# Column tiles of 32 for the masked products, and TensorE's block of 32 steps written out without an inner loop

## The reference

```
def step(St, inp):
    qt, kt, vt, gt, bt = inp
    St = St * jnp.exp(gt)[..., None]
    err = jnp.einsum('bhk,bhkv->bhv', kt, St)
    St = St + bt[..., None, None] * kt[..., None] * (vt - err)[..., None, :]
    ot = jnp.einsum('bhk,bhkv->bhv', qt, St)
    return (St, ot)
_, o = jax.lax.scan(step, S0, (qs, ks_, vs, gs, bs))
```

## Time and profile before

| | us |
|---|---|
| median of 3 runs | 9948.8 |
| lowest, highest of them | 9948.15, 9957.26 |
| the profiled execution: its own time | 9947.83 |
| its span in the trace | 9946.0 |
| TensorE (PE) busy | 9259.0 |
| VectorE (DVE) busy | 7394.6 |
| ScalarE (ACT) busy | 6812.3 |
| GpSimd (POOL) busy | 3586.7 |

### The profile page before, as it was taken

The page is one execution under the profiler, slowest core; times in us unless marked ns, Lnnn a source line. Parts: engine busy times, 40 slices in busy tenths (PEclk is TensorE's granted clock), DMA queues, the critical chain, the costliest instruction groups (busy, mean ns, idle before and its releaser), DMA issues. The chain is left out here.

```text
span 9946.0 us, 369852 instructions
## 1 busy us (share of the span) xinstructions
PE 9259.0 (93%) x137172; PEld 6223.8 (63%) x137172; DVE 7394.6 (74%) x13320; ACT 6812.3 (68%) x15797; POOL 3586.7 (36%) x5963
## 2 busy tenths in 40 slices
PE   4799999999999999999999999999999999997888
PEld 2566666666666666666666666666666666663333
DVE  2688888888888888888888888888888888872111
ACT  1677777777777777777777777777777777771111
POOL 0344434444343443443434444443434344440000
PEclk7899999999999999999999999999999999998999
DMA  0211111111111111111111111111111111110000
GB/s 28 52 39 37 39 36 39 37 38 38 36 38 37 39 37 36 38 37 36 39 37 38 38 37 38 36 39 36 39 37 39 36 38 37 37 53 17 8 8 13
DMA packets 514021, 351.68 MB, mean 35 GB/s; under 512 B 63137, under 2 KB 510753, under 8 KB 512817
## 3 DMA queue, kind: packets, MB, share of 16 engines
q1 hardware_dynamic: 511760, 328.31, 13.1%
q0 software_dynamic: 1088, 4.26, 0.1%
HBM read 289.94 MB, written 42.47 MB: 33 GB/s over the span
## 5 line engine op out<-in xcount | busy, mean ns | idle before, releaser
L1188 POOL TENSOR_TENSOR KB<-KB,tot 128x256 f32<-128x256 f32 x1290 | 998.6, 774 | 3904.0 <-PE bank L601 3903.9
L1256 DVE SCALAR_TENSOR_TENSOR acc<-bank,hp,acc 128x510 f32<-128x510 f32 (+2 forms) x2331 | 1714.4, 744 | 75.4 <-ACT hnew L884 11.8
L554 PE MATMUL bank<-hn,w_qkv 128*128 (+1 forms) x3108 | 1524.3, 613 | 3.1 <-issue 2.8
L1318 DVE COPY_PREDICATED BIG<-masks,bank 128x512 f32<-128x512 int32 x1032 | 1040.1, 1008 | 107.7 <-DVE BIG L1318 55.0
L1363 DVE TENSOR_TENSOR invT<-invT,bank 64x128 f32<-64x128 f32 x2576 | 739.9, 287 | 375.3 <-PE bank L652 355.7
L901 ACT ACTIVATE Zm<-bank 64x128 f32<-64x128 f32 x2576 | 703.6, 273 | 387.4 <-PE bank L628 362.1
L1330 DVE TENSOR_TENSOR QKF<-QKF,tot 128x512 f32<-128x512 f32 x1289 | 906.1, 703 | 1.2 <-PE bank L601 1.1
L601 PE MATMUL bank<-QKF,KB 128*64 128x64 f32 x20640 | 888.0, 228 | 0.9 <-DVE QKF L1336 0.6
L667 PE MATMUL bank<-ident,invT 128*128 128x128 f32 x5152 | 798.1, 277 | 75.7 <-DVE invT L1363 71.0
L667 PEld LDWEIGHTS bank<-ident,invT 128*128 128x128 f32 x5152 | 591.7, 141 | 428.9 <-DVE BIG L1318 264.0
L601 PEld LDWEIGHTS bank<-QKF,KB 128*64 128x64 f32 x20640 | 709.4, 137 | 127.6 <-issue 88.9
(11 more groups left out here) (209 smaller groups left out, 20968.7 us busy)
## 6 DMA issues: line engine op xcount, KB each, us to landing
bb<-beta_rows SPq DMA_DIRECT2D x520, 128.0 KB, 4.1
states<-StC SPq DMA_DIRECT2D x288, 128.0 KB, 1.9
w_qkv<-in_L_attn_wk_dram SPq DMA_DIRECT2D x260, 128.0 KB, 2.2
w_qkv<-in_L_attn_wq_dram SPq DMA_DIRECT2D x260, 128.0 KB, 2.2
w_qkv<-in_L_attn_wv_dram SPq DMA_DIRECT2D x260, 128.0 KB, 2.2
StA<-states SPq DMA_DIRECT2D x259, 128.0 KB, 2.1
w_o<-in_L_attn_wo_dram SPq DMA_DIRECT2D x257, 128.0 KB, 2.1
w_fb<-in_L_attn_f_b_dram SPq DMA_DIRECT2D x260, 64.0 KB, 4.0
```

The lines of the kernel that those rows point to most:

```text
L554: mm = eng.matmul(rows(BK["proj_" + "qkv"[n_]]), w_qkv[:, n_, k, :], hn_v[:, k, :, cols], start=(k == 0), stop=(k == KD - 1))
L1188: eng.tensor_tensor(e_, e_, t_.to_broadcast([P, C, P // (2 * m), m]), ALU.mult).then_inc(ev[f"kb_mul{s}"], 1)
L1256: eng.scalar_tensor_tensor(dst, rows(bk)[:, :, 0:BLK - sh], hp[par][:, w_:w_ + 1], dst, ALU.mult, ALU.add).then_inc(ev[("tap_" if t_ < 2 e ...
L1318: eng.copy_predicated(dst, mk, ps).then_inc(ev[f"lvl_e{s}"], 1)
```

## The change

Levels 0 to 4 and the diagonal are computed as four products for each chunk, each for a quarter of 32 tokens: 128 rows of the array, 32 columns of it, 32 output columns. A level's call has 16 products in place of 8 (32 matmul instructions in place of 16). Blocks of levels 0 to 4 are at most 32 tokens long, so nothing wanted falls outside. The copies of the results are not touched.

```
 for ch in range(C):
-    for h in range(2):
-        rw = slice(h * HALF, (h + 1) * HALF)
+    for q4 in range(4):
+        rw = slice(q4 * QUART, (q4 + 1) * QUART)
         mm = eng.matmul(chains(BK["diag"])[rw, ch, rw], kk[:, ch, rw], q_[:, ch, rw], start=True, stop=True)
...
         if s == LEVELS - 1:
...
+        elif s < LEVELS - 2:
+            for ch in range(C):
+                for q4 in range(4):
+                    rw = slice(q4 * QUART, (q4 + 1) * QUART)
+                    n4 = QUART // (2 * m)
+                    mm = eng.matmul(ps[rw, :, ch, q4 * n4:(q4 + 1) * n4, :], kb[:, ch, rw],
+                                    QKF[par][:, :, ch, rw].rearrange("p f (n two m) -> p f n two m", two=2, m=m)[:, :, :, 1, :],
+                                    start=True, stop=True)
         else:
...
-    loop(eng, step, begin_block, lambda o: close_out(), HTOT // 2)
+    for i in range(-4, 0):
+        step(i, i % 2)
+    with nc.Fori(0, NO, engines=(mybir.EngineType.PE,), hint_back_edge=True) as o:
+        begin_block(o)
+        for k in range(HTOT):
+            step(o * HTOT + k, k % 2)
+        close_out()
```

## The result

The changed kernel takes 9984.95 us (median of 15 runs, 9960.35 to 10003.18) where the kernel before took 9953.75 on the same chip (15 runs, 9939.75 to 9959.27): a ratio of 1.0029, 95% interval [1.0021, 1.0037]. It is slower by 0.3%, where 9750 us was predicted, 2% faster. The profiled execution took 9965.84 us, with a span of 9964.1.

The account below looks back on a forecast made before the run. TensorE (busy 93%) was taken as nearly full, but VectorE's gapless 22 us stretch limits which savings count. 9948 − 113 (products) − 66 (inner branches) − 44 (block ends) + 25 (code) = 9750 us; own range 9700 to 9810, wider 9640 to 9880.

Parts of the forecast that it names:

- The block of products: Levels 0 to 4 and diagonal: each block takes 0.38 us, 0.23 us less, 1.38 us a step over six blocks.
- rivals B: Products: column tiles run only in twos, 0.64 us a block, the product term vanishes, 9878 us; chance 0.13.
- C: Products: a matmul has a price whatever its columns, 0.8 us a block or more, some 10,580 us; chance 0.04.
- What of it reaches the end: Only level 4's and diag's savings, between state(0) and y4, count: 0.44 us a step, 113 us over 256 steps.
- The inner branches: TensorE's loop branches inside a block (L460): eight go, 8.3 us each, 66 us saved.
- The block ends: Close_out to state(1): with the hint, open_out starts earlier and at full clock; 6.3 us seven times, 44 us saved.
- More code: TensorE's instruction fetch: 192 more instructions a step, stops more than double from 19 us, plus 25 us (bounds 0 and 100).
- rival D: Instruction fetch falls behind: a stop in every second step, 340 us, near 10,065 us; decides from 0.8 us a step; chance 0.06.
- the product term: The new blocks of levels 0 to 4 and diagonal: 113 us saved over 256 steps.

Follow-up runs that it names:

- place 0: Also written s0: changed kernel with level 0 in halves as before and the loop's first instruction at place 0 of an instruction packet; 9760.64 us, ratio 0.9805.
- e2: The kernel before, old products kept, with the new loop (32 steps written out, with the hint); 9902.46 us, ratio 0.9948.
- e4: The changed kernel without `hint_back_edge=True`; 9971.94 us, ratio 1.0014.
- places 0 and 64: For 64: the same kernel as at place 0, but the loop's first instruction at place 64 of a packet; 9784.93 us, ratio 0.9829.
- s128: The same kernel as at place 0, but the loop's first instruction at place 128 of a packet; 9953.24 us, ratio 0.9996.
- w2: The kernel s128 with two empty semaphore instructions added to each TensorE step; 10459.61 us, ratio 1.0491.
- w3: The kernel at place 0 with two empty semaphore instructions added to each TensorE step; 9864.59 us, ratio 0.9899.
- v3: The kernel at place 0 with VectorE's `clip_z` made 0.27 us longer, same result; 9881.76 us, ratio 0.9923.

## Why the prediction was wrong

**The block of products** was right: 0.39 us measured, 0.38 taken. Column tiles that share all 128 rows run four at a time, so rivals B (0.64) and C (0.8 or more) are out.

**What of it reaches the end** was right in place and too high in size. The waits of turn 5 and of state(0) grew as forecast, from 0.35 to 0.55 to 0.74 and from 0.32 to 0.40 to 0.76. A step without a stop most often takes 32.44 us in the kernel at place 0 (0.34 less than before, where 0.44 was forecast). In the changed one it takes 32.56 on average where it took 32.81. Over 256 steps that is some 85 us of the 113 at place 0 and 60 in the changed kernel.

**The inner branches**, 66 us, were right: the eight steps that held one went from 40.39 to 32.64 us, 62 us. e2 as a whole, with inner branches and block ends together, brought 54 where these two terms had 110.

**The block ends**, 44 us: missing. The hint did nothing in this kernel, as e4 shows, and the mean step over a block's end went from 43.88 to 43.64 us, 2 us in seven. The prediction had said that no row shows a hint and that this term may be 0.

**More code** is the step that failed. Its term was plus 25 us and measured about 140. "PE stops with nothing awaited, inside products, 40 to 50 us in all" became 139 us in level 0 and 17 in the projections, beside 20 and 1 before, and more that is spread thin. The prediction multiplied the share of extra code by today's stops; its bounds, 0 and 100, came from nothing but that, and it took the stops of the kernel before for chance. They are no chance. There are four or five borders between packets a step. At places 0 and 64 they cost next to nothing: one stop over 1.2 us in 256 steps at place 0, none outside the block ends at place 64. In the changed kernel one costs 2.0 to 3.3 us where it falls in level 0, and 1.2 to 2.1 in the projections. Turning level 0 into 32 dense matmuls made that stretch a larger target (32 more instructions in it), and with 30 instructions over five packets a border comes back to the same place every 256 / 30 = 8.5 steps and then lies in level 0 for about two of them: of 256 steps 52 stopped there. Over the 255 steps from first to last out_product, the two rows of the changed kernel (compare) are:

```profile
386.46 1.99 PE L732 MATMUL bank<-z,w_o 128*128 128x512 f32 x4
...
8933.78 1.98 PE L732 MATMUL bank<-z,w_o 128*128 128x512 f32 x4
```

8933.78 − 386.46 = 8547.3 us, 17 more than before. The shorter step gained 60, the inner branches 62 and the block ends 2, so the stops took some 140. That is rival D, instruction fetch falling behind, at 0.55 us a step: by itself under the 0.8 from which it was to decide, but the hint and some 50 us of the product term were missing as well. Had the stops kept to the 25 us of the sum, 9948 − 60 − 64 + 25 = 9849 us would have been left, inside the range. That the forecast of 9750 is nearly what the change takes with level 0 left alone and its code laid well, 9760.64 us, is a coincidence: in that kernel the hint works and the stops are gone, for reasons that the prediction did not have.

Two of the rivals' sums have slips, on which nothing hangs: with the plus 25 of the stops, 740 us on top give some 10,600 and not 10,580 for C, and 9748 + 340 is 10,088 for D, which is 10,065 only with the stops of before taken off.

**What stays open.** Shown is that the place of a border decides, by s0 against s128 and by w2, and that a packet lands 1.3 to 1.6 us ahead of the end of each stop. Why that packet starts only about when TensorE stops, and why borders at other places cost next to nothing, no run shows; that TensorE needs a stock of slow instructions to bridge the time is an argument. Open is also when the hint works.

## What to carry to other kernels

Where an engine runs blocks of many short instructions, count its instructions a step, count the packets of its instruction queue, and look up where a stop "with nothing awaited" stands: if it moves by a fixed number of instructions from step to step, it is a packet's border, and its price can be worked out for every place it will pass. Then a change that adds instructions is costed by where the borders will fall and not by a share; here the same instructions took from 9761 to 9953 us by place alone. And time that TensorE saves ahead of a wait for VectorE is only had together with VectorE's: moving one instruction of 0.42 us off its full stretch brought 139 us, more than the new blocks did. What a moved instruction brings can differ from its own length, because it changes which instructions meet GpSimd's.

## What the runs showed of the hardware that was not expected

- Four column tiles that share all 128 rows take 0.39 us for 32 matmuls, 12 ns each on average; the starts inside such a block are mostly 6 to 11 ns apart, and weight loads run while matmuls on the same rows are in flight. The Trainium skill, TensorE: Matmul & The Clock Gate, says in its section The mechanism that weight loads overlap matmuls in flight only where the row group differs, and in its section Wait — 56ns, not 53.3ns? that starts are never under some 25 ns apart. The trace disagrees with both.
- In all 52 stops of level 0 an instruction packet lands 1.26 to 1.64 us ahead of TensorE's next matmul, and stops within a block of the loop lie a multiple of 256 instructions apart.
- Two instructions a step that do nothing cost some 500 us at one place (w2) and some 100 at another (w3).
- A hint on a branch was worth 22 us in one kernel and nothing in another with the same branch.
- The same VectorE instruction took 0.69 us or 1.34 us (L1357 in v3), the longer one where GpSimd's L1192 ran beside it; L1351 at place 0 took 0.43 or 1.08 us, again the longer one where L1192 ran beside it.
